# One running sum in DRAM, added to by the experts' scatter, in place of rows weighted and summed at the end

## The reference

```
x = layernorm(x + attention(x))
gates = softmax(x @ gate)                    # 16 experts
keep the 3 largest gates of a token, divided by their sum: g[token, e], else 0
y[token] = sum over e of g[token, e] * (relu(x @ W1[e] + b1[e]) @ W2[e] + b2[e])
out = layernorm(x + y)
```

## Time and profile before

| what | us |
|---|---|
| time, median of 3 | 1911.62 |
| the profiled execution: its own time | 1915.52 |
| its span in the trace | 1913.8 |
| busy in the span: PE, PE's weight loads, DVE, ACT, POOL | 1725.6, 1286.1, 1390.2, 752.6, 1202.2 |
| first gather of the experts' stage (issue) | 1411.69 |
| first and last scatter of it (issue) | 1424.50, 1836.49 |
| first load of combine (issue) | 1840.67 |

### The profile page before, as it was taken

One profiled execution on the slowest core, in us unless ns is written; L12 is line 12 of the kernel. 1 busy time (PEld: TensorE's weight loads), 2 busy tenths in 40 slices (PEclk: granted clock), 3 DMA queues, 4 the chain that ended last, 5 costly groups with the idle time before them and its releaser, 6 DMA issues. The chain is left out here.

```text
span 1913.8 us, 33436 instructions
## 1 busy us (share of the span) xinstructions
PE 1725.6 (90%) x9587; PEld 1286.1 (67%) x9588; DVE 1390.2 (73%) x3237; ACT 752.6 (39%) x1633; POOL 1202.2 (63%) x1128
## 2 busy tenths in 40 slices
PE   5489999999999999999999999998679999999930
PEld 4356666766766676676676667654359999999930
DVE  3358888888888888988888888855964444444448
ACT  3124444444445444444544444444432222222225
POOL 2138778777877777887786787651445555555544
PEclk9679999999999999999999999998569999999975
DMA  9856556755745775565666557506602222222255
GB/s 311 274 166 182 160 166 191 196 154 155 193 139 177 208 209 152 172 171 160 189 203 182 165 144 196 157 1 207 214 30 70 71 69 71 71 69 71 69 189 186
DMA packets 165567, 294.72 MB, mean 154 GB/s; under 512 B 18736, under 2 KB 59440, under 8 KB 165440
## 3 DMA queue, kind: packets, MB, share of 16 engines
q1 hardware_dynamic: 152624, 262.51, 46.5%
q0 software_dynamic: 10752, 29.37, 4.9%
q10 hardware_dynamic: 2064, 1.31, 0.2%
HBM read 190.12 MB, written 102.76 MB: 153 GB/s over the span
## 5 line engine op out<-in xcount | busy, mean ns | idle before, releaser
L735 ACT ACTIVATE prob<-b_ps 128x512 f32<-128x512 f32 (+3 forms) x768 | 354.4, 488 | 367.8 <-PE b_ps L572 267.8
L499 POOL TENSOR_TENSOR acc<-acc,prob 128x1024 f32<-128x1024 f32 (+1 forms) x192 | 352.3, 1835 | 6.4 <-POOL acc L499 3.6
L571 PE MATMUL b_ps<-q,k 128*128 128x512 f32 (+3 forms) x768 | 296.6, 390 | 11.8 <-DMA q<-mrow 7.4
L472 POOL TENSOR_TENSOR roped<-rot 128x512 f32<-128x512 f32 x128 | 174.6, 1364 | 183.6 <-DVE rot L858 182.8
L564 PE MATMUL a_ps<-k,q 128*128 128x512 f32 (+3 forms) x768 | 267.1, 385 | 19.4 <-DMA k<-scratch_hilo 9.0
L840 DVE CUSTOM_DVE_ANT_0 masked<-a_ps,causal 128x128 bf16<-128x128 f32 (+3 forms) x512 | 237.3, 479 | 59.3 <-PE a_ps L564 51.7
L653 PE MATMUL y_ps<-prob,v_sb 128*64 128x512 f32 (+3 forms) x1536 | 276.6, 496 | 0.0
L1551 DVE TENSOR_SCALAR hT<-h_ps,b1T 128x128 f32<-128x128 f32 x448 | 126.1, 344 | 191.2 <-PE h_ps L1470 179.3
L572 PE MATMUL b_ps<-q,k 65*128 65x512 f32 (+3 forms) x768 | 264.8, 348 | 0.0
L888 DVE RECIPROCAL inv<-inv 128x128 f32<-128x128 f32 x256 | 232.2, 929 | 8.5 <-ACT inv L776 6.2
L477 POOL TENSOR_TENSOR lo<-roped,hi 128x512 fp32r<-128x512 f32 x128 | 176.9, 1382 | 85.9 <-ACT hi L748 85.9
(11 more groups left out here) (263 smaller groups left out, 2524.8 us busy)
## 6 DMA issues: line engine op xcount, KB each, us to landing
q<-scratch_hilo SPq DMA_DIRECT2D x192, 256.0 KB, 4.6
k<-scratch_hilo SPq DMA_DIRECT2D x192, 256.0 KB, 5.2
scratch_hilo<-hi SPq DMA_DIRECT2D x64, 512.0 KB, 3.9
scratch_hilo<-lo SPq DMA_DIRECT2D x64, 512.0 KB, 4.5
w_sb<-scratch_wsplit SPq DMA_DIRECT2D x32, 512.0 KB, 3.6
w<-in_L_ffn_W_dram SPq DMA_DIRECT2D x32, 512.0 KB, 9.6
got<-scratch_ys SPq DMA_DIRECT2D x32, 384.0 KB, 6.1
wv_sb<-scratch_wsplit SPq DMA_DIRECT2D x16, 512.0 KB, 6.1
```

Of the source, the lines that this page charges most:

```text
L499: nc.gpsimd.tensor_tensor(sums, old, probs(q), ALU.add).then_inc(m["sum_p"], 1)
L571: nc.tensor.matmul(out, k1[s][:, h, js], q1[s][:, h, qs], start=True, stop=False, skip_group_check=True)
L735: nc.scalar.activation(probs(q)[:, h, :], b_ps[:, h, 0:w], ACT.Exp).then_inc(exp_done[h], 1)
```

## The change

1. The gate weights (16 numbers of a token, zero where an expert isn't chosen) are stored in scratch_xn in front of the token's 256 features, so that a row has 272 numbers. The gather brings both. `wts` is gone.
2. ACT multiplies the expert's result by its gate weight while it copies it out of PSUM; the column of the weight is a register, loaded from `etile` for each tile.
3. scratch_ys is gone. scratch_sum0 has one row per token and 128 spare rows. In routing, SP stores the resident rows (residual and weighted bias) there, 1 MB after each 8 of POOL's additions.
4. The scatter of a tile adds to scratch_sum0. Because two tiles may hold the same token, POOL waits before each scatter until the one before has landed.
5. The ring of gathered rows has 8 places instead of 4; gathers still go 4 tiles ahead. The loops are unrolled by 8 tiles.
6. Combine loads each token's one row (groups of 4, 8, 8, 8, 4 tiles), takes mean and variance, normalizes and stores. POOL has no part in it.

```diff
-XIN = 4
+XIN = 8
+AHEAD = 4
+SUMS = 1
@@ routing, SP, after the loads of the weights
+            sp.wait_ge(m["r_zero"], 1)
+            some = S["zeros"][:].rearrange("p (t d) -> p t d", t=1)
+            for i in range(SUMS):
+                rows = dram[f"sum{i}"].rearrange("(t p) d -> p t d", p=P)[:, TILES if i == 0 else 0:TILES + 1, :]
+                sp.dma_start(rows, some.broadcast_to([P, rows.shape[1], D])).then_inc(S["sums_in"], 16)
+            sp.wait_ge(m["r_g32"], 1)
+            sp.dma_start(dram["xn"].rearrange("(t p) c -> p t c", p=P)[:, :, 0:E_], tmp[:]).then_inc(m["r_gst"], 16)
+            first = dram["sum0"].rearrange("(t p) d -> p t d", p=P)
+            for g in range(GROUPS):
+                sp.wait_ge(m["r_bbadd"], LG * (g + 1))
+                half = S["x1a"] if g < 2 else S["x1b"]
+                sp.dma_start(first[:, g * LG:(g + 1) * LG, :], half[:, g % 2 * LG:g % 2 * LG + LG, :])\
+                    .then_inc(S["sums_in"], 16)
@@ routing, DVE, before the tables are decoded
             dve.wait_ge(m["r_inv"], BATCHES)
+            dve.wait_ge(m["r_gst"], 16)
@@ experts, POOL
-            for t in range(XIN):
+            for t in range(AHEAD):
                 gather(t)
+            pool.wait_ge(S["sums_in"], 16 * (SUMS + TILES // TB))
             for t in range(SLOT_TILES):
-                if t + XIN < SLOT_TILES:
+                if t + AHEAD < SLOT_TILES:
                     pool.wait_ge(m["m_xtr"], done(t))
-                    gather(t + XIN)
+                    gather(t + AHEAD)
                 pool.wait_ge(m["m_ytaken"], done(t))
+                if t >= SUMS:
+                    pool.wait_ge(ys_st[(t - SUMS) % 2], 16 * ((t - SUMS) // 2 + 1))
                 pool.indirect_dma_start(
-                    out=dram["ys"], out_offset=bass.IndirectOffsetOnAxis(ap=dst_i[:, t:t + 1], axis=0),
-                    in_=y[:, t % 2, :], in_offset=None).then_inc(ys_st[t % 2], 16)
+                    out=dram[f"sum{t % SUMS}"], out_offset=bass.IndirectOffsetOnAxis(ap=dst_i[:, t:t + 1], axis=0),
+                    in_=y[:, t % 2, :], in_offset=None, compute_op=ALU.add).then_inc(ys_st[t % 2], 16)
@@ experts, ACT
+                e = act.value_load(etile[0:1, bass.ds(t, 1)], min_val=0, max_val=E_ - 1)
                 act.wait_ge(m["m_y"], done(t))
...
-                nc.scalar.activation(y[:, s, :], yo_ps[:, s, 0:D], ACT.Copy).then_inc(m["m_ytaken"], 1)
+                nc.scalar.activation(y[:, s, :], yo_ps[:, s, 0:D], ACT.Copy, scale=xin[:, place, bass.ds(e, 1)])\
+                    .then_inc(m["m_ytaken"], 1)
@@ combine
+    SIZES = (4, 8, 8, 8, 4)
...
             for g in range(GROUPS):
+                for i in range(SUMS):
+                    sp.dma_start(got[i][:, rows(g), :],
+                                 dram[f"sum{i}"].rearrange("(t p) d -> p t d", p=P)[:, rows(g), :]).then_inc(ld[g], 16)
+            for g in range(GROUPS):
+                sp.wait_ge(m["c_out"], ENDS[g])
+                sp.dma_start(out_v[:, rows(g), :], got[1][:, rows(g), :]).then_inc(m["c_stored"], 16)
+            sp.wait_ge(m["c_stored"], 16 * GROUPS)
...
             for g in range(GROUPS):
                 act.wait_ge(m["c_var"], g + 1)
+                nc.scalar.activation(r[:, 0, rows(g)], mv[:, rows(g), 1], ACT.Sqrt, bias=eps[:, 0:1])\
+                    .then_inc(m["c_std"], 1)
                 act.wait_ge(m["c_rs"], g + 1)
+                for t in range(ENDS[g] - SIZES[g], ENDS[g]):
+                    nc.scalar.activation(got[1][:, t, :], got[0][:, t, :], ACT.Identity, bias=r[:, 4, t:t + 1],
                                          scale=r[:, 3, t:t + 1]).then_inc(m["c_out"], 1)
...
+            moments(0)
             for g in range(GROUPS):
                 if g + 1 < GROUPS:
+                    moments(g + 1)
                 scales(g)
```

More of the change, by code:

```diff
@@ L923, in routing_phase @@
     w1, w2, b1T = S["w1"], S["w2"], S["b1T"]
-    src_i, dst_i, wts, gT, etile, ident = (S[k] for k in "src_i dst_i wts gT etile ident".split())
+    src_i, dst_i, gT, etile, ident = (S[k] for k in "src_i dst_i gT etile ident".split())
     with ExitStack() as ctx:
@@ L1034, in _ @@
         def _(pool):
+            pool.memset(S["zeros"][:], 0.0).then_inc(m["r_zero"], 1)
             pool.memset(tri[:], -1.0).then_inc(m["r_const"], 1)
@@ L1321, in gate_weights @@
                 weigh(tiles_of(GROUPS - 1))
-                V.tensor_tensor(wts[:], top[:, :, 0:TOPK], bc(red[:, 1, :], TOPK), ALU.mult)
                 link(V.tensor_copy(g32[:, :, 0:E_], tmp[:]))
@@ L1573, in combine_phase @@
 def combine_phase(nc, A, dram, S, out):
[L1575 to L1579, removed]
+    SIZES = (4, 8, 8, 8, 4)
+    ENDS = [sum(SIZES[:g + 1]) for g in range(len(SIZES))]
+    GROUPS = len(SIZES)
     with ExitStack() as ctx:
@@ L1582, in sb @@
             return ctx.enter_context(nc.sbuf_tensor(name, shape, dt))
-        got = sb("got", [P, AHEAD, GRP, TOPK * D], F32)
+        got = [sb(f"got{i}", [P, TILES, D], F32) for i in range(2)]
         stats = sb("stats2", [P, TILES, 6], F32)
@@ L1594, in combine_phase, with rows @@
         block = ctx.enter_context(nc.Block())
-        out_v = out.rearrange("b (g t p) d -> (b g) p t d", p=P, t=GRP)
-        ys = dram["ys"][0:NTOK * TOPK, :].rearrange("(k t p) d -> t p k d", k=TOPK, p=P)
+        out_v = out.rearrange("b (t p) d -> p (b t) d", p=P)
+        def rows(g):
+            return slice(ENDS[g] - SIZES[g], ENDS[g])
         @block.sync
         def _(sp):
[L1600 to L1606, removed]
-            for g in range(GROUPS):
[L1608 to L1616, removed]
@@ L1652, in _ @@
                 act.wait_ge(m["c_rs"], g + 1)
-                if g >= 2:
-                    act.wait_ge(st[g % 2], 16 * (g // 2))
-                for i in range(GRP):
-                    t = g * GRP + i
-                    nc.scalar.activation(outb[:, g % 2, i, :], token_rows(S, t), ACT.Identity, bias=r[:, 4, t:t + 1],
+                for t in range(ENDS[g] - SIZES[g], ENDS[g]):
+                    nc.scalar.activation(got[1][:, t, :], got[0][:, t, :], ACT.Identity, bias=r[:, 4, t:t + 1],
@@ L1730, in post_ln_block @@
         S.update(x1a=sb("x1a", [P, 2 * TB, D], F32), src_i=sb("src_i", [P, SLOT_TILES], I32), dst_i=sb("dst_i", [P, SLOT_TILES], I32),
-                 wts=sb("wts", [P, TILES, TOPK], F32),
                  gT=sb("gT", [P, 2 * 512], F32R), etile=sb("etile", [1, SLOT_TILES], I32))
+        S.update(zeros=sb("zeros", [P, D], F32), sums_in=ctx.enter_context(nc.semaphore("sums_in")))
         with ExitStack() as inner:
@@ L1742, in scratch @@
 def scratch(nc):
-    shapes = {"xsplit": [B, P, 2 * DK * T], "wsplit": [PAIRS + PAIRS // 2, P, 2 * DK * 256], "hilo": [2, 2, P, 2, T], "xn": [NTOK, D],
-              "ys": [PLACES * NTOK + SLOT_TILES * P, D]}
+    shapes = {"xsplit": [B, P, 2 * DK * T], "wsplit": [PAIRS + PAIRS // 2, P, 2 * DK * 256], "hilo": [2, 2, P, 2, T], "xn": [NTOK, E_ + D]}
+    shapes.update({f"sum{i}": [NTOK + P, D] for i in range(SUMS)})
     return {k: nc.dram_tensor(f"scratch_{k}", v, F32, kind="Internal").ap() for k, v in shapes.items()}
```

90 lines of the change are left out of this document (23 added, 67 removed).

## The result

The changed kernel takes 1991.4 us (median of 4 runs, 1986.84 to 1993.4) against 1912.05 on the same chip: a ratio of the means of 1.0405, with a 95% interval of 1.0379 to 1.0432. It is slower by about 79 us. Forecast was 1882. The profiled execution took 1993.4 us, its span is 1991.7.

A forecast was written before the change was run, and what follows sets the result against it. PE was taken to bound the experts' stage, with scatter waits hidden. Combine starting at 1844.4 plus 39.7 gave span 1884.1 against 1913.8, or 1882 us against the median; own range 1875 to 1893, 8-in-10 range 1873 to 2005.

The forecast's parts named there:

- The bound before: Experts' stage of the old kernel: PE sets the pace, 3.72 us a tile.
- combine, new: Combine stage: 39.7 us against 73.1, 33.4 us gained, limited by ACT with its serial hand-overs.
- Routing and the copies hidden: Routing, the experts' first tiles and ACT's multiplying copy: 0 us, extra stores and work hidden.
- The wait alone is free while c stays under 3.72: Experts' stage: PE still sets the pace and POOL's wait for the landing costs nothing below 3.72 us.
- c: Experts' stage: the least distance of two scatters when each waits for the one before to land.
- c = 3.5: Scatter chain on POOL: 2.8 us without addition plus 0.7 for reading old rows, taken as 3.5 us.
- The release: POOL's queue in the experts' stage: 0.3 us from a release to POOL's start.
- rival B: Experts' stage: the chain of additions sets the pace, span 1465.6 + 112 c; chance 0.35 beyond 4.1 us.
- The read of 0.7: Adding scatter: reading 128 old rows as a gather does, some 0.7 us, one phase behind the other.
- The lower bound of 2.8: Scatter chain without any addition: plain flight of 2.5 us plus 0.3 release, 2.8 us at least.
- the turn at 4.00: Scatter distance, 0.5 above the forecast value, from which it decides; every further 0.1 us costs 11 us.
- The stage change: From POOL's branch after the last landing to combine's first issue: 1.67 us, as before.

The follow-up runs named there:

- e1: Changed kernel with the same waits, but a plain scatter that overwrites rows instead of adding: 1877.85 us, ratio 0.9833.
- e4: Changed kernel with POOL's two waits swapped, the last scatter's landing before `y`: 1925.42 us, scatters 4.09 us apart.
- e7: Kernel before's combine and tables, without its multiplications; ACT weights rows, plain scatters to three places don't wait for one another: ratio 1.0023.
- e9: Changed kernel with POOL's landing wait first and only the first 8 gathers sent, POOL's `m_xtr` wait kept: 1969.71 us, scatters 4.51 us apart.
- e12: As e9, but POOL's wait for `m_xtr` is dropped too: 1932.27 us, scatters 4.13 us apart.
- e3: Changed kernel, each adding scatter taking only 64 of its 128 rows: 1910.59 us, scatters 3.94 us apart.

## Why the prediction was wrong, step by step

- **The bound before** (PE, 3.72 us a tile) and **combine, new**: right. 39.7 us were worked out and 38.0 measured. The working has two slips: its own terms add up to 6.4 us a group of eight, not to the 6.0 or 6.1 that it counts from 20.3 to 26.4 and 32.4, which would make 40.7; and it takes 1.9 us for hand-overs and small chain where the trace has 1.24 (1984.99 to 1986.23), so that a group of eight takes 5.5. The end has the form that the working gave it: eight copies of ACT 4.04 us, root 0.28, six small steps of DVE, four last copies 2.07.

```profile
1980.77 4.04 ACT L1638 ACTIVATE got<-got,r 128x256 f32<-128x256 f32 x8 [1.28 <-DVE r L1672]
1984.71 0.28 ACT L1634 ACTIVATE r<-mv,eps 128x4 f32<-128x4 f32 x1
1986.23 2.07 ACT L1638 ACTIVATE got<-got,r 128x256 f32<-128x256 f32 x4 [1.23 <-DVE r L1672]
```

- **Routing and the copies hidden**: right. ACT's copy with the multiplier takes 0.47 us instead of 0.38, in its idle time. The gate weights' store takes SP 0.43 us and nobody waits for it; the first gather is at 1410.23 (before 1411.69), the first scatter at 1423.26.
- **The wait alone is free while c stays under 3.72**: right, shown by e1.
- **c = 3.5: this is the step that failed.** It was 2.5 (plain landing) + 0.7 (the read) + 0.3 (release), and 4.72 was measured. Two terms were mis-sized. The issue was kept at the plain 0.99 and is 1.59 to 1.67: +0.6 to 0.7, which makes the landing 2.5 + 0.73 + 0.6 = 3.83, measured 3.8 to 3.9. The release was taken at 0.3 from the earlier trace rows, but of a scatter that carried its one wait; with two waits the landing passed in the step ahead and cost 0.75. The sum is 4.6, which by the prediction's own formula gives 1465.6 + 112 x 4.6 - 2.2 = 1979; the last 0.1 us of c isn't explained. Even with the release at 0.3, as e4 has it, c is 4.09 and the change no gain. The longer issue stood in the text only as a point for rival B, without a price.
- **The read of 0.7**: the size came out, as luck. The engines' time grew by 1.10 - 0.37 = 0.73 us, but no phase of reading stands in front of the writes; the rows go one to a packet instead of four to a packet. How much of the time is the reading of the old rows, no run shows.
- **The lower bound of 2.8** was wrong too: the plain scatter of e1, with the same waits, has 3.15 at its end.
- **The choice inside the bounds.** A term known only to lie between 2.8 and 5.8, with the turn at 4.00 and 11 us per 0.1 beyond it, was put at the lower quarter, because plain transfers overlap their rows. That speaks for the bytes alone, and for plain ones. A slip beside it: a c of 3.2 instead of 3.5 moves the forecast by 1.2 us (four times 0.3), not by less than one.
- **Rival B is what happened**, with one difference: PE idles once a tile for gathered rows, behind the same queue, and not for ACT or `hT`. Its formula, 1465.6 + 112 c, gives 1994.2 with c = 4.72; the span is 1991.7. The Trainium skill's rule in "DMA: Bandwidth & Descriptors", section "Anatomy of one DMA — SWDGE (gpsimd) path", counts some 2.0 us for setup and completion together, plus the bytes; the prediction put the 2.0 behind the end of the issue, which the Trainium skill doesn't say there, and so came to an estimated c of 4.3 and 1945, on the right side by luck. Taken whole, the rule gives an estimated 2.3 us for 128 KB, and the trace nearly agrees for the plain scatter (2.4 from the start of the issue, e1); but it has the receipt as most of the 2.0, where the trace has at most 0.6 behind the last byte. What grew is the issue and the engines' time. The Trainium skill's rule in "Collectives: The Full Stack", section "The bandwidth ceiling: the fold count and why AG ≠ RS ≠ AR", as the prediction weighed it, doubled the 0.37 us; these traces have three times as much.
- **The stage change** was kept at 1.67 us and took 2.82, as POOL's drain grew from 0.97 to 2.43 us: 1.15 us in all, a step that no rival had. It isn't the price of the addition or of the wait: e7, with plain scatters that don't wait, has a drain of 2.27.

What stays open: why the issue of an adding scatter has 1.3 us that don't shrink with rows or columns, why the landing in mid-stage is some 0.2 us longer than at the end, what the longer drain waits for, and by which rule one of several waits is carried by the instruction. A version with one sum that waits only where the next tile belongs to another expert wasn't tried.

## What to carry to other kernels

When an edit makes transfers wait for each other, take the whole loop from landing to landing (issue, bytes, receipt, and how the release reaches the queue) and price each term for the new form of the instruction; if the slack against the bound is smaller than the least certain term, forecast around the turn and not below it. Two targets used in turn cut such a chain for the price of one more addition later. And where an instruction waits for two things, look in the trace which of them it carries: with two waits, naming the late one first was worth 70 us here (e4); with three, the same order didn't do it (e9).

## What the runs showed of the hardware

- An indirect scatter that adds, 128 rows of 1 KB: issue on POOL 1.55 to 1.67 us (plain 0.99), one packet for each row where the plain one moves four rows in a packet (192 packets a tile, gather included, against 96: 21504 and 10752 over 112 tiles), 1.10 us of all engines (plain 0.37), landing 3.8 to 3.9 us from the start of the issue (plain 2.4).
- From a passed landing to POOL's next issue: 0.3 us if the DMA instruction carries the wait, 0.7 to 0.75 if a separate step ahead of it does, as I read the steps. A third wait can decide which (e9 and e12).
- POOL's drain behind the last scatter: 0.97 us before, 2.43 in the changed kernel, 5.70 in e3, and 2.27 with the plain scatters of e1 (one at a time) and e7 (free). So most of its growth comes neither from the addition nor from the wait, and its cause stays open:

```profile
L1416 POOLq DRAIN  x1: 5697/5697/5697, 1865.1 to 1865.1; - x1
```
